# One tile and one block for each step of the relational stage, with tables made beside the projection of relations

## What is computed

```python
h_all = jnp.einsum('nf,rof->rno', x, W).reshape(r, n, h, d)
h_src = h_all[edge_type, src]
h_dst = h_all[edge_type, dst]
scores = jnp.einsum('ehd,hd->eh', h_src, attn_src) + jnp.einsum('ehd,hd->eh', h_dst, attn_dst)
scores = jnp.where(scores > 0, scores, NEG_SLOPE * scores)
amax = jnp.maximum(jax.ops.segment_max(scores, dst, num_segments=n), 0.0)
w = jnp.exp(scores - amax[dst])
denom = jax.ops.segment_sum(w, dst, num_segments=n) + 1e-12
out = jax.ops.segment_sum(h_src * (w / denom[dst])[..., None], dst, num_segments=n)
```

## Time and profile before

| | |
|---|---|
| median of 3 runs | 4223.15 us (4221.75 to 4224.39) |
| the profiled execution | 4219.4 us |
| its span, first to last instruction | 4217.6 us |
| mean granted clock of TensorE | 0.889 of full speed |

### The profile page before, as it was taken

The page is one execution under the profiler, slowest core; times in us unless marked ns, Lnnn a source line. Parts: engine busy times, 40 slices in busy tenths (PEclk is TensorE's granted clock), DMA queues, the critical chain, the costliest instruction groups (busy, mean ns, idle before and its releaser), DMA issues. The chain is left out here.

```text
span 4217.6 us, 67721 instructions
## 1 busy us (share of the span) xinstructions
PE 3496.7 (83%) x17983; PEld 2727.1 (65%) x17984; DVE 2818.7 (67%) x7798; ACT 1935.8 (46%) x5274; POOL 2319.3 (55%) x2470
## 2 busy tenths in 40 slices
PE   8788888888888799799989997877878777866793
PEld 4466666666666699799975444655656555645692
DVE  5499999999999655411112222888888888875456
ACT  2355555555555233233322334666666666636230
POOL 5477777777777155400002222777777777737441
PEclk9899999999999999899999998788887888765896
DMA  6677777777777411111113445555565556534446
GB/s 190 200 210 203 202 206 205 207 205 201 203 207 205 151 40 40 56 35 37 35 55 150 178 178 195 170 175 171 168 178 170 168 168 176 160 107 147 122 133 217
DMA packets 266461, 656.43 MB, mean 156 GB/s; under 512 B 52764, under 2 KB 140984, under 8 KB 250408
## 3 DMA queue, kind: packets, MB, share of 16 engines
q0 software_dynamic: 128768, 394.47, 33.2%
q1 hardware_dynamic: 130328, 251.92, 17.4%
q10 hardware_dynamic: 7056, 6.43, 0.4%
HBM read 521.34 MB, written 131.29 MB: 155 GB/s over the span
## 5 line engine op out<-in xcount | busy, mean ns | idle before, releaser
L278 POOL DMA_INDIRECT attn_KV<-kv_tab,attn_stage x880 | 930.1, 1057 | 279.6 <-issue 252.1
L1846 POOL DMA_INDIRECT rel_V<-h_tab,rel_stage x880 | 833.9, 948 | 309.0 <-issue 229.6
L1949 PE MATMUL rel_SP<-rel_V,rel_OH 128*128 128x264 f32 x1760 | 608.5, 483 | 3.6 <-DVE node L2018 1.7
L379 PE MATMUL attn_QP<-node,attn_OHT 128*128 x1760 | 507.4, 414 | 10.2 <-issue 5.5
L391 PE MATMUL attn_SP<-attn_KV 128*128 128x264 f32 x1760 | 494.7, 407 | 20.9 <-DVE node L493 20.3
L1949 PEld LDWEIGHTS rel_SP<-rel_V,rel_OH 128*128 128x128 f32 x1760 | 372.6, 233 | 75.7 <-ACT rel_OH L1884 10.5
L391 PEld LDWEIGHTS attn_SP<-attn_KV 128*128 128x128 f32 x1760 | 344.9, 201 | 94.8 <-issue 37.7
L2018 DVE TENSOR_TENSOR node<-node,rel_SP 128x264 f32 x880 | 366.0, 416 | 50.5 <-PE rel_SP L1949 28.2
L379 PEld LDWEIGHTS attn_QP<-node,attn_OHT 128*128 128x128 f32 x1760 | 334.1, 203 | 61.3 <-issue 14.6
L1740 PE MATMUL pr_H<-WX,pr_YT 128*128 128x512 f32 x784 | 345.3, 593 | 0.0
L454 DVE TENSOR_TENSOR attn_KV<-attn_KV,attn_QP 128x512 f32<-128x512 f32 x440 | 298.0, 677 | 56.0 <-DMA attn_KV<-kv_tab,attn_stage 55.9
(11 more groups left out here) (393 smaller groups left out, 6761.0 us busy)
## 6 DMA issues: line engine op xcount, KB each, us to landing
rel_OHT<-dst_rows SPq DMA_DIRECT2D x55, 1024.0 KB
h_tab<-pr_H SPq DMA_DIRECT2D x49, 1056.0 KB, 4.0
attn_KV<-kv_tab,attn_stage POOLq DMA_INDIRECT x880, 3.8
rel_V<-h_tab,rel_stage POOLq DMA_INDIRECT x880
pair_Y<-y SPq DMA_DIRECT2D x105, 130.0 KB, 2.1
kv_tab<-qkv_KV SPq DMA_DIRECT2D x49, 256.0 KB, 2.5
mix_Y<-y_out SPq DMA_DIRECT2D x49, 256.0 KB, 4.3
attn_runs<-runs SPq DMA_DIRECT2D x55, 192.0 KB
```

The source lines that it names most:

```text
L278: pool.indirect_dma_start(out=KV[:, i * IT + u, 0:2 * FEAT], out_offset=None, in_=d["kv_tab"][:, :], in_offset=bass.IndirectOffsetOnAxis(a ...
L379: mm = pe.matmul(QP[(2 * i + v) % BANKS][:, (u % 2) * FEAT:(u % 2 + 1) * FEAT], OHT[:, u, :], query(blks[v]), start=True, stop=True)
L1846: pool.indirect_dma_start(out=V[:, i * IT + u, :], out_offset=None, in_=d["h_tab"][:, :], in_offset=bass.IndirectOffsetOnAxis(ap=stage[:, ...
L1949: pe.matmul(SP[(c * IT + u) % SUMS][:, 0:NUMC], OH[:, j * IT + u, :], V[:, j * IT + u, :], start=True, stop=True).then_inc(s["sums"], 1)
```

## The change

The relational stage gets tables of its own, for single steps of one tile and one block: 782 + 48 = 830 steps, padded to 832 (`SINGLES`), so 52 periods in place of 55. These tables are made in `project_relations`, whose loop is written out for that; `project_with_tables` loses what served the relational stage alone (the gathers of edge types, the masks of relations, `dst_rows`, `idx_rel`). The relational tables overwrite `block_of`, `dst_in` and `idx_src`, which the first layer no longer needs. A single step has a block number of its own, so `blocks_of` loads 16 in each period. The front of `project_relations` keeps its two turned halves in one PSUM bank.

```diff
+SINGLES = -(-(TILES + LAST_BLOCK) // IT) * IT
+SINGLES_PAD = SINGLES + IT
...
 def project_with_tables
-                    if t == 17:
-                        sp.wait_ge(p["local"], 1)
-                        sp.dma_start(d["dst_rows"][0:FULL * P, :]...
-                    if t == 42:
-                        sp.wait_ge(p["masked"], MASKS)
-                        sp.dma_start(d["relmask"][:, :], relmask[:, :]).then_inc(p["out"], 16)
...
-                    if 21 <= t < 21 + SGROUPS:
-                        gather(raw["typ"], "typ", t - 21, "typ")
...
-                    if t == 31:
-                        pe.wait_ge(p["links"], 1)
-                        turn("typ", 0, 2)
-                    if t == 32:
-                        pe.wait_ge(p["turned_sb"], 4)
-                        turn("typ", 1, 2)
...
 def project_relations
-        f = norm_front(nc, m, ctx, "pr", BLOCKS)
+        f = norm_front(nc, m, ctx, "pr", BLOCKS, banks=1)
...
+        last_i = pb("last_i", [1, TILES], I32)
+        raw = {n: pb(f"raw_{n}", [P, SGROUPS, P], I32) for n in ("dst", "src")}
+        raw["typ"] = raw["dst"]
+        rawf = pb("rawf", [P, SGROUPS, P], F32)
+        pt = ctx.enter_context(nc.psum_tensor("one_pt", [P, 512], F32))
...
-                pipeline(sp, body, LEAD, 1, BLOCKS)
+                def tables(t):
...
+                    if t == 26:
+                        sp.wait_ge(p["scaled"], 4)
+                        sp.dma_start(d["runs"][0:FULL * P, :]...
...
+                    if t == 41:
+                        sp.wait_ge(p["masked"], MASKS)
+                        sp.dma_start(d["relmask"][:, 0:SINGLES_PAD * RELS], relmask[:, :]).then_inc(p["out"], 16)
+
+                with nc.allow_non_contiguous_dma(reason="one column of the tiles' destinations"):
+                    sp.dma_start(last_i[:, :], d["dst"][0:TILES, P - 1:P].rearrange("t o -> o t")).then_inc(p["last"], 16)
+                for t in iterations:
+                    body(t, t % 2)
+                    tables(t)
...
-                pipeline(dve, body, LEAD, 1, BLOCKS)
+                    if t == -6:
+                        dve.wait_ge(p["last"], 16)
+                        dve.wait_ge(p["iota"], 2)
+                        link(dve.tensor_scalar(last_i[:, :], last_i[:, :], 7, None, ALU.arith_shift_right))
+                        dve.tensor_copy(tile_f[:, :], tile_i[:, :])
+                        link(dve.tensor_copy(last_f[:, :], last_i[:, :]))
+                        dve.tensor_tensor(last_f[:, :], last_f[:, :], tile_f[:, :], ALU.add).then_inc(p["ends"], 1)
+                        dve.tensor_copy(step_f[:, :], step_i[:, :]).then_inc(p["less"], 1)
+                    if t in (-4, -2):
+                        h = (t + 4) // 2
+                        dve.wait_ge(p["ends"], h + 2)
+                        dve.tensor_copy(ends[:, h * HALF:(h + 1) * HALF], pt[:, 0:HALF]).then_inc(p["ends_sb"], 1)
...
+                def turn(n, h, order):
+                    pe.wait_ge(p["rawf"], order + 1)
+                    for k in range(4 * h, min(4 * h + 4, SGROUPS)):
+                        mm = pe.transpose(pt[:, (k - 4 * h) * P:(k - 4 * h + 1) * P], rawf[:, k, :], m.ident[:, :])
+                    mm.then_inc(p["turned"], 1)
...
 def relational_layer
-    G = ITS
+    G = SINGLES // IT
...
-            return nc.values_load_multi_w_load_instructions(m.block_of[0:1, bass.ds(g * PAIRS, PAIRS)], engines=[engine], min_val=0,
+            return nc.values_load_multi_w_load_instructions(m.block_of[0:1, bass.ds(g * IT, IT)], engines=[engine], min_val=0,
...
-                                           m.sd[:, bass.ds(blks[u // 2] * RH, RH)], start=True, stop=True)
+                                           m.sd[:, bass.ds(blks[u] * RH, RH)], start=True, stop=True)
...
-                        acc = m.node[:, bass.ds(blks[u // 2] * NUMC, NUMC)]
+                        acc = m.node[:, bass.ds(blks[u] * NUMC, NUMC)]
```

More of the change, by code:

```diff
@@ L45 @@
 assert CS * CHUNKS == SPAD
+SINGLES = -(-(TILES + LAST_BLOCK) // IT) * IT
+SINGLES_PAD = SINGLES + IT
+assert -(-SINGLES_PAD // P) == SGROUPS and SINGLES_PAD <= SPAD
 BIG = 1e30
@@ L689, in project_with_tables @@
         s = sems(nc, m, "qkv", "w mm q_out kv_out kv_free stored0 stored1")
-        p = sems(nc, m, "prep", "last iota link ends ends_sb less bsel rows jt_turned jt jf jb dst src typ attr sent cleared "
-                 "steps ids block_of rawf turned turned_sb ne tail scaled pl links mixed masked local out")
+        p = sems(nc, m, "prep", "last iota link ends ends_sb less bsel rows jt_turned jt jf jb dst src attr sent cleared "
+                 "steps ids block_of rawf turned turned_sb ne tail scaled pl links mixed out")
         x_in = [new_sem(nc, m, f"qkv_x_in{i}") for i in range(2)]
@@ L821, in _ @@
                 sp.wait_ge(p["block_of"], 16)
-                sp.wait_ge(p["out"], 16 * 8)
+                sp.wait_ge(p["out"], 16 * 5)
             @block.gpsimd
@@ L1580, in project_relations @@
     with ExitStack() as ctx:
+        p = sems(nc, m, "one", "last iota link ends ends_sb less bsel rows jt_turned jt jf jb dst src typ sent cleared "
+                 "steps ids block_of rawf turned turned_sb ne tail scaled pl links mixed masked local out")
         s = sems(nc, m, "pr", "mm sc_mm h_out sc_out d_out stored0 stored1 rows_free "
@@ L1644, in body, with gather, tables @@
                     front_scale(pool, m, f, t + 4, i)
-                pipeline(pool, body, LEAD, 1, BLOCKS)
+                def gather(out, table, k, done):
+                    pool.indirect_dma_start(out=out[:, k, :], out_offset=None, in_=d[table][:, :],
+                                            in_offset=bass.IndirectOffsetOnAxis(ap=tsel_i[:, k:k + 1], axis=0)).then_inc(p[done], 16)
+                def tables(t):
+                    if t == 3:
+                        pool.wait_ge(p["rows"], 1)
+                    if 3 <= t < 7:
+                        for k in (2 * (t - 3), 2 * (t - 3) + 1):
+                            if k < SGROUPS:
+                                gather(raw["dst"], "dst", k, "dst")
+                    if 7 <= t < 7 + SGROUPS:
+                        gather(raw["src"], "src", t - 7, "src")
+                    if t == 14:
+                        pool.wait_ge(p["rawf"], 1)
+                        pool.wait_ge(p["steps"], 64)
+                    if 14 <= t < 14 + SGROUPS:
+                        gather(raw["typ"], "typ", t - 14, "typ")
+                pool.iota(tile_i[:, :], pattern=[[1, TILES]], base=0, channel_multiplier=0).then_inc(p["iota"], 1)
+                pool.iota(step_i[:, :], pattern=[[P, SGROUPS]], base=0, channel_multiplier=1).then_inc(p["iota"], 1)
+                for t in iterations:
+                    body(t, t % 2)
+                    tables(t)
             @block.scalar
@@ L1711, in _ @@
+                dve.memset(sent[0:1, 0:1], -1)
+                dve.memset(sent[0:1, 1:2], 1 << 20).then_inc(p["sent"], 1)
+                dve.memset(ids[:, FULL, :], 0).then_inc(p["cleared"], 1)
+                for t in iterations:
+                    body(t, t % 2)
+                    tables(t)
             @block.tensor
@@ L1855, in restage @@
                     if has(k, G):
-                        act.copy(stage[:, i * IT:(i + 1) * IT], m.idx_rel[:, bass.ds(k * IT, IT)]).then_inc(s["staged"], 1)
+                        act.copy(stage[:, i * IT:(i + 1) * IT], m.idx_src[:, bass.ds(k * IT, IT)]).then_inc(s["staged"], 1)
                 def near(k, q):
```

264 lines of the change are left out of this document (222 added, 42 removed).

## The result

The changed kernel took 4172.7 us (median of four runs, 4165.0 to 4180.3) beside 4222.5 for the kernel before in the same session: a ratio of 0.9881, with an interval from 0.9863 to 0.9900. Forecast were 4170 us, in a range from 4159 to 4192. The profiled execution is the longest of the four, 4180.3 us with a span of 4177.7, so its stages are read one by one and not as a sum.

The account below looks back on a forecast made before the run. POOL's issue of gathers was taken to bound the relational stage, PE the projection. Terms -60.1 + 1.0 + 2.5 + 6.0 - 3.0 = -53.6 us gave 4169.5 by the median, forecast 4170; 8-in-10 range 4159 to 4192.

Parts of the forecast that it names:

- Gathers, -60.1: Relational stage: 832 gathers in place of 880, 48 x 1.252 us less, if POOL stays the bound.
- Registers, +1.0 at the end and hidden otherwise: Relational stage: loads of 16 values and more addresses hide under DVE's landing wait; +1.0 us behind the last gather.
- The rival in which the work becomes the chain: DVE and PE in each relational period: register work all exposed, 2.7 us a period, 4251 us; chance 0.04.
- the one in which 1.6 us a period come through: Relational stage: register work partly exposed, period 20.5 us, DVE 26 us late at the end, 4196 us; chance 0.10.
- PE in the projection, +2.5: `project_relations`: 21 turns and two small products at 0.11 us each on a full PE add 2.5 us.
- Lead-in, +6.0: Start of `project_relations`: DVE waits for the last destinations, first gathered row 6.0 us later (bounds 4 and 8).
- my two readings: Lead-in of `project_relations`: the 782 elements take 3.3 us as forecast, or 2.2 if engine count sets the rate.
- ring order: SP's queue in the projection's lead-in: descriptors consumed in order, so the last destinations' load stands behind 2 MB of weights.
- Stalls by the tables, 0: `project_relations`: new table work and transfers hidden in blocks of 7.5 us, cost 0.
- The rival of 16 us: `project_relations`, SP's queue: tables stall it as they do the earlier stage, 16 us, 4186 us; chance 0.12.
- Loop written out, 0: `project_relations`: PE is already full in the loop, so writing it out changes 0.
- The earlier stage, -3.0: `project_with_tables` loses table work: turns -0.8, masks' store -0.7, gathers and stores -1.5 us.

Follow-up runs that it names:

- again: The changed kernel once more with no edit: 4174.1 us, ratio 0.9879 to the kernel before.
- last_first: Changed kernel with SP issuing the load of the tiles' last destinations ahead of the heads and the weights: 4170.3 us, ratio 0.9866.
- before_unrolled: The kernel before with only the loop of `project_relations` written out on all five engines: 4226.2 us, ratio 1.0004.
- before_52: The kernel before with 52 relational periods in place of 55, leaving out the last 48 steps: 4164.2 us, ratio 0.9848.
- last_second: Changed kernel with SP issuing the load of the last destinations between the heads and the weights, on another chip: 4560.0 us, ratio 0.9861.
- last_on_act: Changed kernel with the load of the last destinations issued from ScalarE's queue at the stage's start, on another chip: 4568.9 us, ratio 0.9878.
- dve_thrice_again: Meant as the changed kernel with three block-number loads on DVE; extra loads were dropped in building, so the changed kernel itself, another chip: 4562.4 us, ratio 0.9866.

## Why the forecast was right, term by term

**Gathers, -60.1.** POOL stayed the bound: no wait over 0.3 us. The term was mis-sized by 4.3 us, since 832 gathers took 1.2574 us each and not 1.2522. The trace shows where most of them lie: single gathers of 1.0 to 1.18 us in place of 0.946, 37, 32 and 33 of 832 in the profiles of the changed kernel, `again` and `last_first`, and 8 to 15 in those of `before_unrolled`, the kernel before and `before_52`. So they go with the changed kernel and not with the number of steps; which part of it makes them is open. `before_52` is 2.8 us longer in its gathers by another sign, a median of 949 ns. Priced from it, three periods less are worth 58.1 and not 60.1 us.

**Registers, +1.0 at the end and hidden otherwise.** The load took 1.10 us, the upper bound of 0.93 to 1.10 (0.06 us for each value more), and was exposed by 0.50 us a period more, as forecast. It was hidden, but the cover was another than I named: the landing wait fell by 0.10 us a period, not by 0.6, and DVE's two waits for PE by 0.23 and 0.12. The end cost 1.3 us by the first profile (33.8 us from the last gather to the last addition, 32.5 before), 2.1 beside `before_52`. The rival in which the work becomes the chain and the one in which 1.6 us a period come through are excluded by the 3.6 to 5.6 us that all of it costs together. How much more DVE could have taken was not measured.

**PE in the projection, +2.5.** 2.7 measured, 2.0 to 2.4 of them turns at 0.09 to 0.11 us.

**Lead-in, +6.0.** 7.4 measured, within 4 to 8; it spreads, since the first row comes 14.8 to 15.9 us behind the first transfer in the seven profiles of the changed kernel and 8.0 to 8.3 in three with the old tables. The operations took 2.6 us, not 3.2; the load was used 12.6 us after the first issue of the weights, where I had 10.7. The transfers by SP's queue show where those 1.9 us are. These are the kernel after, from 2213 to 2214 us, to 2215, and from 2217 to 2218, in packets, MB and share:

```profile
q1 hardware_dynamic: 51, 0.42, 99.5%
...
q0 software_dynamic: 78, 0.23, 56.9%
q1 hardware_dynamic: 139, 0.12, 36.0%
...
q1 hardware_dynamic: 173, 0.00, 17.4%
```

The queue is full until 2214 and has 0.12 MB left after it, so the weights end at about 2214.3, 7.6 us behind their issue and not 6.7 as in the earlier trace rows (2202.6 to 2209.3): 0.9. The elements go on through the slice from 2217 (8 packets come after 2217.85), some 3.6 us behind the weights where I took 3.3: 0.3. The rest is the landing, 1.3 us in place of 0.65: 0.7. By themselves the 782 elements take 2.6 us (`last_second`): of my two readings the 2.2 us were nearer for the load alone, the 3.3 us for the load behind the weights.

I also explained the wait by ring order. Rows like the earlier trace rows fit that, but `last_on_act` shows that order is not needed for it: the elements are slow beside the weights in a queue of their own too.

**Stalls by the tables, 0.** PE was full (364.8 of 365 us). The rival of 16 us did not come about: blocks of 7.5 us gave the table work its cover. **Loop written out, 0:** shown by `before_unrolled`.

**The earlier stage, -3.0.** The last copy of keys and values starts at 170.0, 168.8 and 169.4 us in the profiles of the changed kernel, `again` and `last_first`, and at 173.9, 173.7 and 176.0 in those of the kernel before, `before_52` and `before_unrolled`. The stage gave about 5 us by the means (169.4 and 174.5), 3.7 to 7.2 from single profile to single profile: more than I took and, by the means, inside the -1.5 to -7. Which of its parts gave more I didn't separate.

**Between the projection and the relational stage, not in the sum.** 0.7 us more from the last store to the first gather, alike in every profile of the changed kernel. Its reason was not sought.

The errors cancelled in part: gathers +4.3, lead-in +1.4, the passage between the stages +0.7 and the end +0.3 on one side, the earlier stage about -2 on the other. 4172.7 is 2.7 us from 4170; with medians loose by some 4 us, that nearness is in part luck. The prediction's own range, 4158 to 4181, isn't what its bounds add up to, which is 4162.5 to 4182 around 4169.5; the measured time lies in both.

The versions with the load moved ahead of the weights gave 3.5 and 4.1 us of the projection back (404.3 and 403.7 us from its first transfer to its last store, in place of 407.8 on either chip). In whole times neither can be told from the changed kernel (0.9866 and 0.9879, with intervals of 0.0015 on each side). So no version was shown to beat it.

## What to carry to other kernels

When the gap between issues fills an engine's line from first to last, count instructions on that engine and little else: 48 fewer gathers gave 58 us, and all that came with single steps, doubled register work on two engines included, cost 3.6 to 5.6. A small transfer that a stage's first step waits for was late beside a large one, behind it in one queue and in a queue of its own. Issue it ahead of the large one in the same queue, and then look for what the small one delays in turn. Before a doubled cost is read from a time, count its instructions in the trace.

## What the runs showed that I had not expected

- The same kernels took 9 to 10% longer on two other chips. By the page of `dve_thrice_again` the gathers of the relational stage were issued 1.48 us apart and not 1.257, though one took 0.96 us as against 0.95, and PE's granted clock was lower (0.78 after 0.82, below). Busy time by stretch of that execution, attention, projection and relational stage:

```profile
180.00:1500.00 1320.00, 1010.84 (x4590) 767.07 (x4588) 1106.39 (x2494) 655.32 (x1743) 940.08 (x853) 0.88 0.64 181
2450.00:2770.00 320.00, 320.00 (x950) 156.59 (x949) 85.96 (x310) 110.57 (x211) 86.33 (x131) 1.00 0.51 193
2900.00:3900.00 1000.00, 737.37 (x3047) 534.54 (x3046) 720.21 (x1909) 524.50 (x1407) 653.40 (x678) 0.78 0.50 146
```

  In that stage POOL does wait for PE's sums (74.6 us in 60 waits, up to 2.2 us each), so its issue is no longer the only bound. Over the whole stage 148 of the 831 gaps between gathers are longer than 0.32 us, where the first chip has none, and they hold 177 of the 186 us by which the gathers take longer. The additions to `node` on DVE are as long as on the first chip (0.419 us after 0.416 in the mean), and PE's products for the sums are longer (0.517 after 0.479). The change still gave 1.3 to 1.6%. Whether the lower clock (0.78 against 0.82, 0.88 against 0.95) is cause or effect was not tested.
- In the attention stage one gather takes up to 1.9 us, and 269 to 284 of 880 take over 1 us in the six profiles of the first two sessions. The count differs from execution to execution of one kernel (283 and 270 in the first profile and `again`), and with it the stage's gathers by 7.3 us, of the 7.8 between these two executions. Of the 283, 251 ran while DVE did the multiplication of L473, which runs beside 466 of the 880. No run separates the two, so that it makes them long is not shown.
- 782 separate elements of 4 bytes, issued ahead of the weights in the same queue, were in use 5.2 us after their issue.
